# A two-layer perceiver on one core: straight program, front norms in two parts, the back chain's first statistics taken by the front chain

## What is computed

```python
x = x + xattn0(layernorm(x), ctx, ctx)   # 16 heads, 16 gathered keys each
x = x + attn0(layernorm(x))              # weights from distances of 3-D positions
x = x + moe(layernorm(x))                # shared expert and 2 of 8 routed experts
x = x + xattn1(layernorm(x), ctx)        # self, cross, feed-forward, 3 norms
x = x + attn1(layernorm(x))              # differential attention over heads, feed-forward
x = x + peer(layernorm(x))               # product keys, top 16 of 16 x 16, gelu

def _layernorm(x, axis=-1, eps=1e-05):
    m = jnp.mean(x, axis=axis, keepdims=True)
    v = jnp.var(x, axis=axis, keepdims=True)
    return (x - m) / jnp.sqrt(v + eps)
```

## Time and profile before

| what | value |
|---|---|
| median of 3 runs | 3246.67 us (3242.1 to 3248.07) |
| profiled execution, device time | 3243.26 us |
| its span, first to last instruction | 3241.5 us |
| VectorE, ScalarE, GpSimd busy | 1823.8, 893.7, 897.4 us |
| instructions in the trace | 48228 |
| moved by DMA | 392.65 MB |

### The profile page before, as it was taken

How to read it: one execution, slowest core, us unless ns; L and a number is a source line. 1 busy time by engine, 2 the same in 40 slices (tenths; PEclk the granted TensorE clock), 3 DMA queues, 4 the chain that set the end, 5 groups by cost and what they waited for, 6 DMA issues and landing times. The chain is left out here.

```text
span 3241.5 us, 48228 instructions
## 1 busy us (share of the span) xinstructions
PE 2508.1 (77%) x16640; PEld 1861.0 (57%) x16640; DVE 1823.8 (56%) x7134; ACT 893.7 (28%) x1985; POOL 897.4 (28%) x1108
## 2 busy tenths in 40 slices
PE   5786899758985799948997689858899489885645
PEld 3575568645673558735685456745587356862432
DVE  2313456654657547474567546575574745665457
ACT  0212233222421234222332224212342223322211
POOL 0002114322243233241143222431332411423052
PEclk8598899978997899978999789978999789996767
DMA  6075236140552425332361405524153323612100
GB/s 233 13 271 189 90 105 227 64 151 38 162 178 68 176 72 197 108 122 87 105 227 64 154 35 160 178 68 178 64 195 118 117 92 105 227 64 109 26 0 7
DMA packets 215097, 392.65 MB, mean 121 GB/s; under 512 B 83728, under 2 KB 167952, under 8 KB 189616
## 3 DMA queue, kind: packets, MB, share of 16 engines
q1 hardware_dynamic: 208688, 372.49, 33.6%
q0 software_dynamic: 6144, 16.79, 1.6%
HBM read 350.55 MB, written 38.67 MB: 120 GB/s over the span
## 5 line engine op out<-in xcount | busy, mean ns | idle before, releaser
L543 POOL TENSOR_TENSOR rstdB<-veB,mhalf 128x2 f32<-128x2 f32 (+1 forms) x112 | 81.3, 726 | 899.8 <-DVE veB L1482 886.3
L891 PE MATMUL ps<-xbT,stream 128*128 128x128 f32 x2560 | 314.0, 276 | 9.6 <-DMA stream<-in_experts 9.1
L891 PEld LDWEIGHTS ps<-xbT,stream 128*128 128x128 f32 x2560 | 303.1, 192 | 26.3 <-DMA stream<-in_experts 14.3
L301 POOL TENSOR_TENSOR hTB<-pb,sbuf 128x2048 f32<-128x2048 f32 x32 | 152.3, 4771 | 378.8 <-DVE pb L1873 378.8
L1116 PE MATMUL ps<-ident,work 128*50 128x128 f32 x32 | 12.0, 375 | 198.2 <-POOL work L647 141.1
L904 PE MATMUL ps<-stream,hTA 128*128 128x256 f32 x640 | 153.0, 382 | 15.7 <-issue 11.3
L891 PE MATMUL ps<-xbT,ctxA 128*128 128x128 f32 x1280 | 157.8, 276 | 2.0 <-DMA ctxA<-in_experts 1.9
L891 PEld LDWEIGHTS ps<-xbT,ctxA 128*128 128x128 f32 x1280 | 151.4, 192 | 10.8 <-DMA ctxA<-in_experts 4.8
L1711 DVE TENSOR_TENSOR hTA<-ps,hTA 128x512 f32<-128x512 f32 x120 | 82.2, 685 | 129.2 <-PE ps L891 129.2
L1140 PE MATMUL ps<-aTB,w1a 128*128 128x256 f32 x512 | 127.4, 393 | 25.8 <-ACT work L1417 24.2
L1295 ACT COPY yb<-ps 128x256 f32<-128x256 f32 x120 | 44.3, 369 | 364.9 <-PE ps L904 364.9
(11 more groups left out here) (288 smaller groups left out, 5829.1 us busy)
## 6 DMA issues: line engine op xcount, KB each, us to landing
stream<-in_experts SPq DMA_DIRECT2D x88, 1024.0 KB, 5.2
stream<-in_experts SPq DMA_DIRECT2D x88, 512.0 KB, 6.1
ctxA<-in_experts SPq DMA_DIRECT2D x40, 1024.0 KB
work<-in_ctxT SPq DMA_DIRECT2D x32, 1028.0 KB, 7.2
hTB<-in_ctxN SPq DMA_DIRECT2D x32, 1024.0 KB, 7.0
down<-in_experts SPq DMA_DIRECT2D x40, 512.0 KB
ctxA<-in_ctxT SPq DMA_DIRECT2D x16, 1024.0 KB, 8.9
stream<-in_ctxT SPq DMA_DIRECT2D x16, 1024.0 KB, 11.1
```

Of the source, the lines that this page charges most:

```text
L301: return e.tensor_tensor(out.rearrange("p (a d h) -> p a d h", a=8, d=16), a.unsqueeze(2).broadcast_to([P, 8, 16, 16]), vals[:, t, :].rear ...
L543: nc.gpsimd.tensor_tensor(rstdB[:, span(tag, p)], veB[:, span(tag, p)], mhalf[:, 0:len(PARTS[tag][p])], ALU.pow).then_inc(pool_done, O.ste ...
L891: ins = mm(ps[:, 2 * (b % 2) + u, f * P:(f + 1) * P], wu[:, u, k, f * P:(f + 1) * P], xbT[:, b % 2, k, :], start=k == 0, stop=k == KT - 1)
```

## The change

Seven things are done together.

- The loop is a Python `for`: seven passes are written out, with constant addresses.
- `xA` and `xB` are exchanged from pass to pass, so the copy at the end is gone.
- The statistics of `y0` (`mvY`), its epsilon and its root (`rstdY`) come at the end of the front chain, ahead of the last `x6` add. `y0` itself starts with `mr` and the scalings.
- `out_done` is outside the cleared semaphores. A pass no longer ends with a wait for its output; instead VectorE and ScalarE wait for it before they overwrite `xnB`, and SyncE only at the very end.
- `n1` and `n2` go in parts of three tiles and one; all four tiles are scaled on VectorE. `n1` and `n2` take two slots fewer each.
- `with_bias` on GpSimd takes gain and bias adds of a tile in turn rather than four and four.
- `ORDER` is a new string of 188 slots instead of 192.

The diff, cut to its core:

```diff
@@ PARTS, TURNED
-        PARTS = dict.fromkeys(("y1", "y2"), (range(T - 1), range(T - 1, T)))
+        PARTS = dict.fromkeys(("y1", "y2", "n1", "n2"), (range(T - 1), range(T - 1, T)))
+        TURNED.update(dict.fromkeys(("n1", "n2"), ((0, 0), (1, 0)) * 2))
@@ group
+            xA, xB = (x_odd, x_even) if g % 2 else (x_even, x_odd)
@@ SyncE, end of a pass
-                    if "b" in streams:
-                        sp.wait_ge(out_done, 16 * T)
+                    if g == G:
+                        sp.wait_ge(out_done, 16 * T * G)
@@ GpSimd, front
+                        for p in range(2):
+                            rstd("n1", p)
+                            yield
+                        with_row("n1", 1)(1)
...
+                        pool.wait_ge(vec_done, V["y0", "var"])
+                        nc.gpsimd.tensor_tensor(rstdY, veA, mhalf[:, 0:T], ALU.pow).then_inc(pool_done, O.step("y0", "rstd"))
@@ TensorE, front, first block
+                            if i == T + 1:
+                                for t in PARTS["n1"][0]:
+                                    turn_norm("n1", t, xnA, TURNED["n1"][t])
                             yield
...
-                        yield from norm("n1", xnA, (0, 1))
+                        for t in PARTS["n1"][1]:
+                            turn_norm("n1", t, xnA, TURNED["n1"][t])
+                        yield
@@ VectorE, front, first block (the second block likewise with n2)
+                            if i == T + 1:
+                                scaled_part("n1", 0, xA, xnA)
                             if i >= 2:
...
                                 stats("n1", xA, smallA, t)
-                            yield
-                        yield from norm("n1", xA, xnA, smallA, turned="n0", early=True)
+                            if i >= T:
+                                variance("n1", i - T)
+                            yield
+                        scaled_part("n1", 1, xA, xnA)
+                        yield
@@ VectorE, end of the front
+                        for t in range(T):
+                            v.wait_ge(vec_done, V["acc", t, NPICK - 1])
+                            vv.bn_stats(stA[:, t, :], xA[:, t, :]).then_inc(vec_done, V.step("y0", "st", t))
+                        for t in range(T):
+                            v.wait_ge(vec_done, V["y0", "st", t])
+                            vv.bn_aggr(mvY[:, t, :], stA[:, t, :]).then_inc(vec_done, V.step())
+                        own_steps()
+                        vv.tensor_scalar(veA, mvY[:, :, 1], EPS, None, ALU.add).then_inc(vec_done, V.step("y0", "var"))
                         yield
@@ VectorE, start of the back
-                        yield from norm("y0", xB, xnB, smallB)
+                        yield
+                        if g >= 2:
+                            v.wait_ge(out_done, 16 * T * (g - 1))
+                        vv.scalar_tensor_tensor(mrB, mvY[:, :, 0], -1.0, rstdY, ALU.mult, ALU.mult).then_inc(vec_done, V.step("y0", "mr"))
+                        for t in range(HALF):
+                            vv.tensor_scalar(xnB[:, t, :], xB[:, t, :], mvY[:, t, 0:1], rstdY[:, t:t + 1], ALU.subtract,
+                                             ALU.mult).then_inc(vec_done, V.step("y0", t))
@@ end
-                    if "f" in streams:
-                        own_steps()
-                        vv.tensor_copy(xB, xA).then_inc(vec_done, V.step())
...
-        with nc.Fori(1, G) as g:
+        for g in range(1, G):
```

More of the change, by code:

```diff
@@ L689, in norm, with turn_norm @@
                         yield
-                    def turn(tag, t, src, place):
+                    def turn_norm(tag, t, src, place):
                         bank, c = place
@@ L1616, in front @@
                                 stats("n2", xA, smallA, t)
+                            if i >= T:
+                                variance("n2", i - T)
                             yield
-                        yield from norm("n2", xA, xnA, smallA, turned="n1", early=True)
+                        scaled_part("n2", 1, xA, xnA)
+                        yield
                         v.wait_ge(pe_done, PE["router"])
```

127 lines of the change are left out of this document (78 added, 49 removed).

## The result

The changed kernel takes 3171.4 us (median of 4 runs, 3163.0 to 3173.2), the kernel before 3247.4 us (4 runs): a ratio of 0.9763, 95% interval 0.9742 to 0.9784. It is faster by 76 us; the forecast was 3184 us in a range from 3130 to 3220 us. Compared again beside the experiments, on another occasion, the same kernel came out at 3188.5 us and 0.9826 (0.9791 to 0.9862). The forecast lies between the two.

The account below looks back on a forecast made before the run. A pass was taken as bound by its matmul order for 337 us, then by VectorE's chain for 41 us. Terms 32.4 + 6.5 + 21 = 60 us off 3243.3 gave 3183, forecast as 3184 us, range 3130 to 3220.

Parts of the forecast that it names:

- Part 1, the jump: At the loop's end: writing the loop out removes 6 jumps back, 2.9 us each.
- Part 2, statistics moved: End of the front: `x6` ends 1.5 us later; barrier releases VectorE some 1.75 us after `x6`.
- Part 3, output wait: Start of a pass: output lands by about 2 us, so the new wait on VectorE and ScalarE costs 0 to 0.3 us.
- Boundaries: From `x6` to first scores: 4.9 us saved at six looped boundaries, 3.0 at the last, 0 at the first; 32.4 us.
- Part 4, front alone: Norms in parts before the first pass: 2.9 us at the first norm, 3.6 at the second, together 6.5 us.
- Part 5, the passes: Norms in parts and new order inside seven passes: net 3.0 us a pass, 21 us; bounds 2 lost to 10 gained a pass.
- First norm: Front's first norm in a pass: one TensorE gap and half of another close, with smaller ones, 2.5 us a pass.
- Second norm with the layer norm behind it: In a pass, eight turns now stand ahead of the end of `w2x`, on which the layer-norm chain hangs: 0.9 us lost.
- rival B: Half-clock stretch of a pass vanishes too, as filled gaps keep the clock up: 52 us more, 3130 us; chance 0.13.
- A: The forecast itself, whole kernel: 3184 us; chance 0.50.
- Rival D: Slower: front turns held back by VectorE stall TensorE in the passes, 5.25 us a norm, 74 us, 3257 us; chance 0.07.
- Rival C: Only boundaries and front alone gain; the order's gain is taken back at the layer-norm wait: 3204 to 3220 us; chance 0.30.

Follow-up runs that it names:

- parts 1 to 3: Kernel before with loop written out, buffers exchanged, output wait moved, first back norm's statistics and root at the front chain's end: 3223.5 us, 0.9940.
- the first profile: Profile of the changed kernel at its first measurement, against the kernel before: 3171.4 us, 0.9763.
- in the second: Profile of the same changed kernel, measured again beside the experiments on another occasion: 3188.5 us, 0.9826.

## Why the prediction was right, and where it was not

The sign and the size (60 us forecast, 76 and 54 measured) were right, and so were most of the places. Step by step:

- **Part 1, the jump: right.** 2.9 us each forecast, 3.1 measured, 19 us by itself.
- **Part 2, statistics moved: right that it pays little, its working wrong.** `x6` comes 1.2 us later, not 1.5. But the step "the barrier then releases VectorE at 0.7 + 1.02" failed: I took the barrier's 1.02 us from a place where GpSimd had long been idle. The root ends 0.8 us after `x6` (0.7 forecast), but then GpSimd takes 1.4 us until it enters the barrier, so that is through at 3.0 us. Root behind the barrier: 1.4 us.
- **Part 3, output wait: right at 0.** No engine waits for it anywhere. What I did not see is that the old wait would have been free as well: it ends under GpSimd's 3.0 us. On the output itself: in the kernel with only the loop written out, SyncE's wait and the barrier end 3.2 us after the issue at 1784.43. Less the 1.0 to 1.4 us of a barrier, the output lands in some 2 us, an estimate. It agrees with the fixed cost of about 2 us that the Trainium skill gives (DMA: Bandwidth & Descriptors, "Anatomy of one DMA"; the section is on transfers issued by GpSimd, this one is issued by SyncE). By that rule the wait would have cost something, but the first scaling comes later still, 2.6 us after `x6` at the earliest.
- **Boundaries: 32.4 us forecast, about 27 measured.** Six of 13.4 - 7.8 - 1.2 = 4.4 us (forecast 4.9), the last 10.4 - 7.25 - 1.2 = 2.0 (forecast 3.0), and the first, forecast at 0, lost 1.5 (from the last `acc` add to the scores 9.0 us before, 10.5 now). All three are the mis-sized barrier. In the times these gains are partly taken back by passes at a lower clock: parts 1 to 3 together gave 0.9940, 19 us, no more than the jump.
- **Part 4, front alone: right for what it reasoned about.** From the first norm's turns to the projection 3.1 us are gone (forecast 2.9). At the second, from the end of the last projection to the router it was 5.25 us and is 3.0: 2.2 us (forecast 3.6). On top came 1.6 us each on `cmat` and the router, which ran partly or wholly at the high clock; with 0.7 us ahead of them, the router ends 9.2 us sooner, not 6.5. The experts' stage, 5.8 us, is a difference between executions.
- **Part 5, the passes: right in sign and near in size, by another way.** With the late `x6` set aside, a pass was to gain 3.0 us; it gained 4.4 in the first profile and 2.6 in the second. First norm: 2.5 forecast, 3.2 and 1.5 measured. `w1a`: 1.4 forecast, 2.7 in both, of which 1.7 are idle time that is gone. Second norm with the layer norm behind it: -0.9 forecast, -1.1 and -1.5 measured (the four `w1x` matmuls taken out of both stretches).
- **The step of part 5 that failed** is "I count one gap and half of the other" at the first norm. The gap ahead of the score transposes did not close, it grew from 1.28 to 1.54 us (and 1460.74 above); it ends with VectorE's `ri`, which the front's steps put ahead on TensorE do not bring sooner. The 1.37 us at the turns went, but others of 0.2 to 0.8 us came. From 33 to 88 us TensorE's idle time sums to 11.6 us a pass before, 11.1 in the first profile after and 10.5 in the second: 0.5 and 1.1 us, not 2.5. The rest of the 3.2 us is the same matmuls taking less time, since less of the stretch is at the low clock. I had left that to rival B.
- **The layer-norm chain was right:** the last `w2x` ends 1.5 us later from the same point, and TensorE still waits 3.2 us at the chain's turns; the wait of 0.39 us at the second norm's turns, which I took to go, is still there. Idle time from 88 to 160 us grows by 1.0 us a pass, in the fourth pass by waits on VectorE that were not there or were shorter (the last row below is the old one):

```profile
1517.66 3.62 PE L1054 MATMUL ps<-w2x,hTB 128*128 128x256 f32 x16
...
1526.92 0.41 PE L935 MATMUL ps<-cum,ones 128*128 128x40 f32 x2 [0.42 <-DVE cum L1683]
...
1532.19 3.70 PE L879 MATMUL ps<-aTA,stream 128*128 128x512 f32 x8 [0.69 <-DVE hTA L1689]
1539.08 1.01 PE L713 MATMUL ps<-ident,sbuf 128*128 128x128 f32 x4 [3.19 <-DVE sbuf L1526]
```

- **Rival B was half true.** I set it against A as all or nothing. In fact the clock stays up in some passes and not in others, with the same code: two of seven in the first profile, none in the second; before the change it was 0.76 to 0.91. A pass at 0.97 takes 358 us, one at 0.82 about 364, and the time of this kernel is a mixture: the passes of the two profiles differ by 12 us in sum, the experts' stage by 6. B's mechanism, that filled gaps keep the clock up, is not shown: the gap that it names stayed, and the clock stayed up through it in some passes and fell in others. The Trainium skill (TensorE: Matmul & The Clock Gate, "A second HAM failure mode: psum-queue depth-cycling") says that small idle times between groups of matmuls make the clock swing. A swing is what the traces show, with such idle times, but not that these decide it: the changed kernel's passes at 0.97 have 11.6 us of idle time from 33 to 88 us, its passes at 0.82 have 10.5.
- **Rival D was wrong:** in the fourth pass TensorE waits 0.2 and 0.4 us for the front's turns. **Rival C** was wrong for the changed kernel, but its 3204 to 3220 us hold for the kernel with parts and old order.
- **Not foreseen:** the back alone is 2.2 us longer (293.1 us from scores to `x6` against 290.9; 292.6 to 295.2 in every kernel without the loop, 290.9 in the one with loop and new order). Four matmuls of the first scores take 1.2 us at the low clock and 0.68 at the high one; before, they change 4.1 us after the first turn (at 2944.09), now only after about 8 us (first turn at 2871.55), within the last row below. Timelines of TensorE, before and after:

```profile
2946.45 1.23 PE L949 MATMUL ps<-aTB 128*128 128x128 f32 x4
2948.15 0.68 PE L949 MATMUL ps<-aTB 128*128 128x128 f32 x4 [0.48 <-DVE pb L1733]
```

```profile
2877.29 1.20 PE L974 MATMUL ps<-aTB 128*128 128x128 f32 x4 [0.27 <-DVE pb L1797]
...
2879.37 1.06 PE L974 MATMUL ps<-aTB 128*128 128x128 f32 x4
```

What decides that stays open.

The order is worth more than I gave it at `w1a`. With parts but the old order a pass takes 366.7 us, with the new order 362.1 and 363.9 us (all three with the late `x6`), and 2.9 us of that difference are the `w1a` stretch.

So the 70 us of the first profile are about 27 at the boundaries (32 forecast), 9 in the front alone (6.5), 31 in the passes (21), 6 of an experts' stage that differs between runs, and -2 in the back alone. The terms are off in both directions. That their sum comes within 16 us of both measurements, and the first norm near its 2.5 us though its gaps stayed, is in part luck.

## What to carry over

A barrier costs from the last operation of its slowest engine: before you move work to the end of a section to hide it, look at what its engine needs to enter the barrier, and put such work right behind it if it fits there. Look for an in-order engine that holds a ready operation behind a wait (here a copy of 0.37 us behind an exponential): exchanging two lines took 26 us out of TensorE's waits and gave 25 to 46 us, at least a third of what the whole change gave. Where the clock swings between passes of one program, one profile is one draw: take a second one on another occasion before you explain a few us of a pass. When you compare a stretch of two orders, count the instructions in it first (here four matmuls changed sides and made 3.2 us look like 5.0), and when you fill a gap, look in the trace whether it is gone.

## What the runs showed of the hardware

- A loop's jump back, taken, held VectorE for 3.1 us; SyncE issued its first load 2.5 us before VectorE started (1803.05 and 1805.54 in the kernel before). The same branch not taken, and straight code entered for the first time, cost none of it.
- GpSimd needs 1.4 us after its last operation before it can enter a barrier (DRAIN rows of 2469 ns with a root of 1.04 us in them, 1779 ns with an operation of 0.36 us).
- The granted clock is not a function of the program: in one execution passes of identical instructions, with the same wait of 1.54 us ahead of the same matmuls, ran at 0.97 and at 0.82 through the same 57 us.
- The experts' stage of the front alone, which waits for transfers, took 84 to 93 us, for kernels with the same transfers there (84.7 and 90.4 us in two profiles of one kernel).
